# Two experts in one tile: a mixture-of-experts layer in 36 tiles of 2 x 128 rows in place of 40 tiles of 256

## What is computed

```python
logits = flat_x @ W_router + b_router
top_vals, top_idx = jax.lax.top_k(logits, TOP_K)          # TOP_K = 2 of 8 experts
...                                                        # softmax over the two
for e in range(NUM_EXPERTS):
    h = jax.nn.relu(flat_x @ W1[e] + b1[e])                # 128 -> 512
    y = h @ W2[e] + b2[e]                                  # 512 -> 128
    w = router_weights[:, e] * expert_mask.astype(x.dtype)
    final_output = final_output + y * w[:, None]
```

## Time and profile before

| | |
|---|---|
| median of 3 runs | 763.26 us (760.21 to 765.3) |
| profiled execution | span 865.4 us, 17483 instructions; no other time of this execution is given |
| TensorE busy | 578.2 us (67%) |
| VectorE, ScalarE, GpSimd busy | 418.2 us (48%), 234.8 us (27%), 340.6 us (39%) |
| mean granted TensorE clock | 0.797 of full speed |
| chain that ended last | PE 35%, DVE 20%, issue 16%, unknown queue 11%, POOL 8%, DMA 4%, ACT 3% |

### The profile page before, as it was taken

How to read it: one execution, slowest core, us unless ns; L and a number is a source line. 1 busy time by engine, 2 the same in 40 slices (tenths; PEclk the granted TensorE clock), 3 DMA queues, 4 the chain that set the end, 5 groups by cost and what they waited for, 6 DMA issues and landing times.

```text
span 865.4 us, 17483 instructions
## 1 busy us (share of the span) xinstructions
PE 578.2 (67%) x5468; PEld 451.0 (52%) x5469; DVE 418.2 (48%) x1454; ACT 234.8 (27%) x411; POOL 340.6 (39%) x424
## 2 busy tenths in 40 slices
PE   2588765233598988882798887667572047999970
PEld 1256544011387877772454665545351026888860
DVE  5774777663232323234884668266173811222225
ACT  1220011220043343343521554233241111222220
POOL 6122046476045454555400000612515665555660
PEclk9786957655799999997699997567555578999995
DMA  7801001131222222232754353232204112222219
GB/s 209 225 25 37 13 26 40 35 125 53 72 71 67 62 65 62 69 119 68 231 172 125 97 151 105 75 99 50 57 8 141 37 49 76 69 69 73 75 43 291
DMA packets 73195, 76.52 MB, mean 88 GB/s; under 512 B 12984, under 2 KB 61368, under 8 KB 73064
## 3 DMA queue, kind: packets, MB, share of 16 engines
q1 hardware_dynamic: 58504, 50.98, 21.3%
q0 software_dynamic: 10224, 22.40, 8.4%
q10 hardware_dynamic: 4400, 2.26, 0.9%
HBM read 46.15 MB, written 29.34 MB: 87 GB/s over the span
## 4 chain that ended last, share of the span: by engine, by line
PE 35%; DVE 20%; issue 16%; another core or an unknown queue 11%; POOL 8%; DMA 4%; ACT 3%; SPq 2%; DVEq 1%; ACTq 0%; POOLq 0%
PE PS L758 31%; POOL ys L528 5%; DMA work<-ys 2%; DVE XN L1340 2%; DVE work L1314 2%; POOL xs L517 2%; DVE stats L1319 2%; DVE work L1729 2%; DVE X L1314 1%; DVE rtmp L1314 1%; POOL turn L526 1%; PE PS L939 1%; PE PS L1089 1%; DVE mv L1322 1%
## 5 line engine op out<-in xcount | busy, mean ns | idle before, releaser
L517 POOL DMA_INDIRECT xs<-pack,adr_i x80 | 79.1, 988 | 235.3 <-ACT pack L1164 154.2
L758 PE MATMUL PS<-w,work 128*128 x1152 | 145.7, 280 | 14.0 <-ACT work L1212 6.5
L528 POOL DMA_INDIRECT ys<-work x144 | 141.0, 979 | 34.1 <-issue 34.1
L758 PEld LDWEIGHTS PS<-w,work 128*128 128x128 f32 x1152 | 135.5, 193 | 25.0 <-issue 24.0
L758 PE MATMUL PS<-work,w1h 128*128 128x256 f16 x576 | 101.9, 278 | 22.7 <-issue 14.1
L1212 ACT ACTIVATE work<-PS,b 128x256 f32<-128x256 f32 x160 | 62.6, 477 | 117.1 <-PE PS L758 93.1
L1314 DVE TENSOR_TENSOR work<-PS,work 128x256 f32<-128x256 f32 (+3 forms) x82 | 33.0, 404 | 121.7 <-issue 75.5
L758 PE MATMUL PS<-work 97*64 97x256 f16 (+5 forms) x608 | 75.5, 318 | 17.2 <-DVE work L1446 10.9
L758 PE MATMUL PS<-work,w1l 128*128 128x256 f16 x288 | 79.9, 278 | 0.6 <-issue 0.6
L758 PEld LDWEIGHTS PS<-work 97*64 97x64 f16 (+2 forms) x608 | 57.8, 165 | 28.4 <-DVE work L1446 13.5
L758 PEld LDWEIGHTS PS<-work,w1h 128*128 x576 | 53.5, 99 | 31.7 <-issue 25.8
(11 more groups left out here) (261 smaller groups left out, 877.3 us busy)
## 6 DMA issues: line engine op xcount, KB each, us to landing
work<-xs SPq DMA_DIRECT2D x132, 65.0 KB
work<-ys SPq DMA_DIRECT2D x12, 512.0 KB, 5.9
k_parts<-work SPq DMA_DIRECT2D x24, 128.0 KB
w<-k_parts SPq DMA_DIRECT2D x8, 384.0 KB
work<-k_parts SPq DMA_DIRECT2D x32, 96.0 KB
work<-q_parts SPq DMA_DIRECT2D x8, 384.0 KB
work<-q_parts SPq DMA_DIRECT2D x32, 96.0 KB
ys<-work POOLq DMA_INDIRECT x144
```

What stands on the lines that cost most here:

```text
L517: g.indirect_dma_start(xs[l], bass.IndirectOffsetOnAxis(adr_i[:, k, T:T + 1], 0), pack_of(l, c)[:, s, k, :].bitcast(U32), None)\
L528: g.indirect_dma_start(ys[l], bass.IndirectOffsetOnAxis(xin[:, q, u, :].bitcast(U32)[:, D:D + 1], 0), yrow[:, q, u, :], None).then_inc(ff[ ...
L758: return t.matmul(o, lhsT, rhs, start=start, stop=stop, skip_group_check=True)
```

## The change

The first layer's counts are rounded up to 128 instead of 256, so its rows take at most 8192/128 + 8 = 72 half tiles, 36 tiles. The two halves of a tile can have different experts, and `eidx_i` holds an expert for each half. What depends on the expert is done for each half in layer 0: `up` has 24 matmuls of 128 columns for 12 of 256, ScalarE eight Relus of 128 columns for four of 256, VectorE two bias additions for one; TensorE, ScalarE and VectorE read two numbers a tile. TensorE's `round_` reads the numbers of tile q ahead of up(q) and keeps them in registers for down(q), in both layers, so that `down` no longer reads them again, except that each round reads those of its predecessor's last tile. 36 is no multiple of 8: a shorter round of 4 tiles follows the loop in layer 0, and the semaphore values are counted anew (`uses`, `nth`). SyncE's padding stores have 128 rows.

```diff
-TILES = (SLOTS // TILE + E, SLOTS // TILE)
+TILES = ((SLOTS // P + E) // 2, SLOTS // TILE)
...
+        odd = [TILES[l] % XS_LEAD for l in range(2)]
+        before = [[0] * XS_LEAD, [rounds[0] + (q < odd[0]) for q in range(XS_LEAD)]]
+        half0 = [0, TILES[0] // 2]
...
+        def nth(l, i, q):
+            return i * (XS_LEAD // 2) + (q // 2 + half0[l])
...
-                r = sp.value_load(tail_i[0:1, e:e + 1], min_val=0, max_val=XS_ROWS - TILE)
-                sp.dma_start(xs[0][ds(r, TILE), :].rearrange("(u p) n -> p u n", p=P), padt[:, e, :, :].bitcast(U32)).then_inc(tails, 16)
+                r = sp.value_load(tail_i[0:1, e:e + 1], min_val=0, max_val=XS_ROWS - P)
+                sp.dma_start(xs[0][ds(r, P), :], padt[:, e, 0, :].bitcast(U32)).then_inc(tails, 16)
...
                     for c in range(FC):
-                        o = PF[:, (2 + 2 * v) * 512 + c * TILE:(2 + 2 * v) * 512 + (c + 1) * TILE]
-                        for k, (w, h) in enumerate(((w1h, 0), (w1h, 1), (w1l, 0))):
-                            ins = mm(o, w[:, ds(e * FF + c * P, P)], xgT[:, v, h, :], start=k == 0, stop=k == 2)
+                        for r in range(len(e)):
+                            n_ = TILE // len(e)
+                            o = PF[:, (2 + 2 * v) * 512 + c * TILE + r * n_:(2 + 2 * v) * 512 + c * TILE + (r + 1) * n_]
+                            for k, (w, h) in enumerate(((w1h, 0), (w1h, 1), (w1l, 0))):
+                                ins = mm(o, w[:, ds(e[r] * FF + c * P, P)], xgT[:, v, h, r * n_:(r + 1) * n_],
+                                         start=k == 0, stop=k == 2)
...
-                                     w2[:, ds(e * FF + c * D, D)], start=c == 0, stop=c == FC - 1)
+                                     w2[:, ds(e[u % len(e)] * FF + c * D, D)], start=c == 0, stop=c == FC - 1)
...
-                def expert(tile):
-                    return pe.value_load(eidx_i[0:1, l, ds(tile, 1)], min_val=0, max_val=E - 1)
+                def expert(i, q):
+                    return [pe.value_load(eidx_i[0:1, l, ds((i * XS_LEAD + q) * 2 + u, 1)], min_val=0, max_val=E - 1)
+                            for u in range((2, 1)[l])]
...
+                def round_(i, first, width_, last):
+                    e = None if first else expert(i - 1, XS_LEAD - 1)
+                    for q in range(width_):
...
-                        up(i, q, expert(i * XS_LEAD + q))
+                        e_next = expert(i, q)
+                        up(i, q, e_next)
                         if q >= 1:
-                            down(i, q - 1, expert(i * XS_LEAD + q - 1))
+                            down(i, q - 1, e)
                         elif not first:
-                            down(i - 1, XS_LEAD - 1, expert(i * XS_LEAD - 1))
+                            down(i - 1, XS_LEAD - 1, e)
+                        e = e_next
...
                         for c in range(FC):
-                            ins = a.activation(hid[:, v, c, :], PF[:, b * 512 + c * TILE:b * 512 + (c + 1) * TILE],
-                                               ACT.Relu, bias=b1[:, ds(e * FC + c, 1)], scale=1 / WSCALE)
+                            for u in range(2):
+                                o = b * 512 + c * TILE + u * P
+                                ins = a.activation(hid[:, v, c, u * P:(u + 1) * P], PF[:, o:o + P],
+                                                   ACT.Relu, bias=b1[:, ds(e[u] * FC + c, 1)], scale=1 / WSCALE)
...
-            act.wait_ge(ff["stored"][XS_LEAD - 1], STORED * rounds[0])
+            for q in range(XS_LEAD):
+                act.wait_ge(ff["stored"][q], STORED * uses(0, q))
...
-                        e = dve.value_load(eidx_i[0:1, l, ds(i * XS_LEAD + q, 1)], min_val=0, max_val=E - 1)
-                        tt(yrow[:, q, :, :], y, bc(b2b[:, ds(e * D, D)], 1, 2), ALU.add).then_inc(f["biased"][0], 1)
+                        for u in range(2):
+                            e = dve.value_load(eidx_i[0:1, l, ds((i * XS_LEAD + q) * 2 + u, 1)], min_val=0, max_val=E - 1)
+                            ins = tt(yrow[:, q, u, :], y[:, u, :], b2b[:, ds(e * D, D)], ALU.add)
+                        ins.then_inc(f["biased"][0], 1)
```

More of the change, by code:

```diff
@@ L298, in build, with uses @@
         rounds = [TILES[l] // XS_LEAD for l in range(2)]
-        before = [0, rounds[0]]
+        odd = [TILES[l] % XS_LEAD for l in range(2)]
+        before = [[0] * XS_LEAD, [rounds[0] + (q < odd[0]) for q in range(XS_LEAD)]]
+        half0 = [0, TILES[0] // 2]
+        def uses(l, q):
+            return before[l][q] + rounds[l] + (q < odd[l])
+        def nth(l, i, q):
+            return i * (XS_LEAD // 2) + (q // 2 + half0[l])
         y_sum = sem("y_sum")
@@ L331, in y_slot @@
                 return rows, x_in[c], 48
-            return yc[:, c % 4, :, :, :], ff["xin"][c % 4], 32 * (before[1] + rounds[1] - 1) + 16 * (c // 4 + 1)
+            return yc[:, c % 4, :, :, :], ff["xin"][c % 4], 32 * (uses(1, c % 4) - 1) + 16 * (c // 4 + 1)
         head_in = [(scat[0][u], 16 * CT_TILES * TOPK * (NC // 4)) for u in range(4)]\
@@ L347, in expert_tiles @@
                 step(0, q)
-            with engine.Fori(1, TILES[l] // XS_LEAD) as i:
+            with engine.Fori(1, rounds[l]) as i:
                 for q in range(XS_LEAD):
                     step(i, q)
+            for q in range(odd[l]):
+                step(rounds[l], q)
         def tiles(c):
@@ L641, in step @@
                 def step(i, q):
-                    wait(sp, ff["stored"][q], (i + before[l]) * STORED)
+                    wait(sp, ff["stored"][q], (i + before[l][q]) * STORED)
                     load_rows(sp, l, i * XS_LEAD + q, q)
@@ L653, in experts @@
                 for q in range(XS_LEAD):
-                    sp.wait_ge(ff["stored"][q], STORED * (before[l] + rounds[l]))
+                    sp.wait_ge(ff["stored"][q], STORED * uses(l, q))
             def y_load(l, c):
@@ L918, in experts @@
                 f, i0 = ff, before[l]
+                n = rounds[l]
                 pe.wait_ge(w1_lo[l], E)
@@ L934, in gather @@
                     else:
-                        pe.wait_ge(f["xin"][q], (i + i0) * 32 + (0 if l == 1 and q < HEAD else 32))
+                        pe.wait_ge(f["xin"][q], (i + i0[q]) * 32 + (0 if l == 1 and q < HEAD else 32))
                     o = PS[:, v, 0:TILE].bitcast(F16).rearrange("p (h u n) -> p h u n", h=2, u=2)
@@ L959, in down @@
                             ins = mm(PS[:, 6 + v, u * D:(u + 1) * D], hid[:, v, c, u * P:(u + 1) * P],
-                                     w2[:, ds(e * FF + c * D, D)], start=c == 0, stop=c == FC - 1)
+                                     w2[:, ds(e[u % len(e)] * FF + c * D, D)], start=c == 0, stop=c == FC - 1)
                     ins.then_inc(f["y"][v], 1)
-                def expert(tile):
-                    return pe.value_load(eidx_i[0:1, l, ds(tile, 1)], min_val=0, max_val=E - 1)
-                def round_(i, first, last):
-                    for q in range(XS_LEAD):
+                def expert(i, q):
[4 more added lines that the diff above has]
+                    for q in range(width_):
                         late = first and (q == 0 or l == 1 and q == HEAD0 - 1)
-                        if q < XS_LEAD - 1:
+                        if q < width_ - 1:
                             if not late:
@@ L974, in round_ @@
                             gather(i + 1, 0)
-                        up(i, q, expert(i * XS_LEAD + q))
+                        e_next = expert(i, q)
+                        up(i, q, e_next)
                         if q >= 1:
-                            down(i, q - 1, expert(i * XS_LEAD + q - 1))
+                            down(i, q - 1, e)
                         elif not first:
-                            down(i - 1, XS_LEAD - 1, expert(i * XS_LEAD - 1))
+                            down(i - 1, XS_LEAD - 1, e)
+                        e = e_next
                         if late:
                             gather(i, q + 1)
-                n = TILES[l] // XS_LEAD
+                    if last:
+                        down(i, width_ - 1, e)
                 gather(0, 0)
[L985 to L989, removed]
+                round_(0, True, XS_LEAD, False)
+                with pe.Fori(1, n - (odd[l] == 0)) as i:
+                    round_(i, False, XS_LEAD, False)
+                if odd[l] == 0:
+                    round_(n - 1, False, XS_LEAD, True)
+                else:
+                    round_(n, False, odd[l], True)
             experts(0)
@@ L1200, in experts @@
             def experts(l):
-                f, i0 = ff, before[l]
+                f = ff
                 act.wait_ge(table, l + 1)
@@ L1661, in round_ @@
                             result(i - 1, XS_LEAD - 1)
-                rounds_ = TILES[l] // XS_LEAD
+                    if last:
+                        result(i, width_ - 1)
+                n_ = rounds[l]
                 parts(0, 0)
```

(7 more changed lines are left out.)

35 lines of the change are left out of this document (19 added, 16 removed).

## The result

Forecast: 779 us, range 755 to 802. Measured: **806.31 us** (803.69 to 807.29, 4 runs) against 763.51 us before, ratio 1.056 with a 95% interval of 1.052 to 1.061. Slower, as forecast, by 43 us where the forecast had 16, and 4 us above the range.

A forecast was written before the change was run, and what follows sets the result against it. TensorE's sequencer, level with its matmuls at 3.3 us a tile, was to become the bound at 5.0 us. Stage +17.7, first and last tile +2, tails -0.5, layer 1 -3: +16 on 763.3, 779 us, range 755 to 802.

The forecast's parts named there:

- the -3 us of the sum: Layer 1: reading the expert's number once a tile, not twice, saves 3 us, bounds 0 and -8.
- 35 intervals x 5.0 = 175.0 us for 157.3: Layer 0's expert stage: 36 tiles paced by TensorE's sequencer replace 40 tiles at 4.03 us, +17.7 us.
- -0.5: Shorter padding stores on SyncE and a table of 72 columns for 80 save 0.5 us at most.
- The stalls in pairs: Layer 0's expert stage: tiles seen going in pairs of 8.2 us, with GpSimd's four scatters behind each other.
- the 0.7 us of "slack": Layer 0: time lost per tile, 4.03 us against the 3.32 us TensorE needs in layer 1.
- the pair rival: Layer 0's tile pairs set the pace, 9.0 us a pair after the change: 762 us, no change; chance 0.13.
- the forecast with the profile's gap: Case where unprofiled execution lacks the pair stalls: today's tile nearer 3.4 us, in all +41, 804 us.
- The low case: Cheap bound: address operations cost only their own 46 and 32 ns, tile 4.1 us, in all -15: 748 us.
- the +2 us for first and last tile: Added latencies of the other engines' work lie on the path only at these two tiles: +2 us.
- The pace stays: Rival: added work fits in the slack and pairs, tiles stay at 4.03 us: 745 us; chance 0.14.
- Weight loads show: Rival: 128-column matmuls in the up-projection can't hide 98 ns weight loads, 5.07 us a tile: 782 us; chance 0.07.
- The clock's 0.04: Chance 0.04 given to the clock rival; its sign was a clock well below 0.99 in the stage.

The follow-up runs named there:

- the run with halves alone: Kernel before, with the up-projection of both layers in 24 matmuls of 128 columns at the same addresses as before: 770.09 us, ratio 1.009.
- the second profile of before: Kernel before, unchanged, run again for another profile: span 759.9 us, time 761.67 us.
- the two runs above with the number read once in the kernel before: Kernel before, TensorE reading a tile's expert number once: 761.74 us; the same plus padding stores waiting only for their own rows: 757.49 us.
- the run of four more operations: Kernel before, with second-half down-projection addresses from a second register holding the same expert's number, 16 address operations a tile for 12: 797.61 us, ratio 1.043.
- the sorted version: Changed kernel with 36 tiles sorted: 32 one-expert tiles run the old code, the last four run the two-expert code; padding stores wait less: 749.22 us, ratio 0.980.

## Why the prediction was wrong

**What held.** The matmuls would no longer cover the sequencer, and a tile would take 5.0 us: 5.03 in the profile. It is 4.9 within the rounds and 7 at their starts, where the branch of 0.5 us wasn't priced, so the last digit is luck. The price of an address operation, 0.12 us by its spacing, is 0.10 to 0.12 by three pairs of runs. The doubled work of ScalarE and VectorE lay beside TensorE (803.56 without it, 806.31 with it). The halves cost nearly nothing on the array: 0.1 us a tile in the run with halves alone, at 0.056 us a matmul. Layer 1 gained: the GELUs of its 32 tiles span 114.2 us (615.8 to 730.0) in the second profile of before and 111.2 (659.7 to 770.9) after, the -3 us of the sum. That is one profile of each; the two runs above with the number read once in the kernel before show 112.8 and 112.9.

**What failed: "35 intervals x 5.0 = 175.0 us for 157.3".** The first term was right, the subtrahend wrong: 39 intervals take 133.1 us in an undisturbed execution, so the term is +43 and not +17.7. With the other terms of the sum (+2, -0.5, -3) it would have given 804.8 us. The forecast had this case in its own text, with 3.4 us a tile and 804 us, but carried the sum "over unscaled". The sign was on the first page of the profile: a span 102 us, 13%, over the median. The stalls in pairs, the 0.7 us of "slack" and the pair rival belonged to that one execution. The engine-bound tile of 3.32 us in layer 1, level with the sequencer's 3.3, was the number to subtract; it needed no second profile. The range says that it holds "the forecast with the profile's gap", but its own figure for that case was 804, above its edge of 802. The low case leans on the disturbed stage too: "35 x 4.1 - 157.3 = -14" would be 35 x 4.1 - 133 = +10 against the undisturbed one.

**The small terms.** "-0.5" for the padding stores and the table was nothing: in the undisturbed profile the last scatters end the wait ahead of the stage, not the stores (the last scatter starts at 198.8 us and has landed at 201.2, the last store is issued at 192.4). The first addition is at 216.2 for 215.1: 1.1 of the +2 us for first and last tile.

**The rivals.** "The pace stays" fell with the run of four more operations, 32 us longer: there was no room at all. "Weight loads show" fell with the halves alone, 7 us longer. The pairs weren't there. The clock's 0.04 stood for a low granted clock all through the stage, and no run shows one: it was 0.97 of full speed there for 1.00 in the undisturbed profile of before, so it hardly took part.

## What to carry to other kernels

In these runs an address made from a run-time number costs TensorE's sequencer about 0.11 us, and it counts against the matmuls of the same stream: here 12 address operations and two number reads a tile were level with 3.3 us of matmuls, and each further one came out of the total at full price. When the sequencer is the bound, what it does once a round (a branch, numbers read again) is paid in full too, here 2 us each time. So keep the operands that need a new address few and wide, and gather what differs into the few tiles that need it, as the sorted version does. Before a sum is made against a profile, compare its span with the median: if it is far above, take paces from the stretches where the bound engine runs without a gap.

## What the runs showed of the hardware that was not expected

- One profiled execution of the kernel before was 13% longer as a whole (a span of 865.4 us for a median of 763.26), with tiles in pairs of 8.2 us for 3.4 us each, while the span of the same program's other profile is within 2 us of its time.
- The spacing of address operations (0.12 us) is two to four times their recorded duration (32 to 46 ns), and the spacing is what the total pays.
- Weight loads whose records last 98 ns hide behind fp16 matmuls of 128 columns to a pitch of 0.056 us, at a granted clock of 1.00 (24 in a row, in the run with halves alone).
